# The feed-forward blocks of a group ahead of the output rows of the preceding group

## The reference

```
h = shift_token(x)
mu = h.mean(-1, keepdims=True)
var = h.var(-1, keepdims=True)
h = (h - mu) / jnp.sqrt(var + 1e-05) * lg + lb
h = h @ w1 + b1              # 256 -> 2 x 682
a, g = jnp.split(h, 2, axis=-1)
h = a * jax.nn.gelu(g, approximate=False)
x = x + h @ w2 + b2          # 682 -> 256
```

## Time and profile before

| | |
|---|---|
| median of 3 runs | 2665.61 us (2664.37 to 2666.09) |
| the profiled execution | 2666.19 us |
| its span, first to last instruction | 2664.4 us |
| mean granted TensorE clock, share of full speed | 0.992 |
| PE busy | 2590.7 us, 97% |
| DVE, ACT, POOL busy | 72%, 64%, 54% |
| feed-forward of layer 0 | about 1210 to 1608 us of the span |
| feed-forward of layer 1 | about 2264 us to the end |

### The profile page before, as it was taken

The page is one execution under the profiler, slowest core; times in us unless marked ns, Lnnn a source line. Parts: engine busy times, 40 slices in busy tenths (PEclk is TensorE's granted clock), DMA queues, the critical chain, the costliest instruction groups (busy, mean ns, idle before and its releaser), DMA issues.

```text
span 2664.4 us, 71388 instructions
## 1 busy us (share of the span) xinstructions
PE 2590.7 (97%) x25088; PEld 2225.2 (84%) x25088; DVE 1919.9 (72%) x3779; ACT 1703.1 (64%) x4184; POOL 1426.1 (54%) x1512
## 2 busy tenths in 40 slices
PE   7999999979999999999999998999999999999998
PEld 5888888768888888887888887888888888888887
DVE  7777777668888778786555556887788887666664
ACT  4666666658778777774444445877777877444442
POOL 7888888567777776662000006777777665000000
PEclk9999999989999999999999999999999999999999
DMA  2111111111111111112111111111111111222221
GB/s 48 37 48 38 43 38 35 42 45 39 50 41 47 41 39 38 57 50 70 56 49 59 53 36 43 40 49 41 49 39 39 40 59 36 79 76 74 78 77 40
DMA packets 167250, 130.39 MB, mean 49 GB/s; under 512 B 24870, under 2 KB 165320, under 8 KB 167093
## 3 DMA queue, kind: packets, MB, share of 16 engines
q1 hardware_dynamic: 164789, 119.81, 14.7%
q0 software_dynamic: 2304, 8.47, 1.1%
HBM read 77.47 MB, written 50.33 MB: 48 GB/s over the span
## 4 chain that ended last, share of the span: by engine, by line
PE 70%; DVE 12%; ACT 11%; issue 5%; POOL 1%; DMA 1%; DVEq 0%; ACTq 0%; SPq 0%; POOLq 0%
ACT attn_E L1103 8%; PE const_banks L1393 6%; PE const_banks L1394 6%; PE const_banks L1395 6%; PE const_banks L1401 3%; PE const_banks L1403 3%; PE const_banks L1402 3%; DVE attn_neg_top L1305 3%; DVE attn_ss L1295 3%; DVE attn_rot_b L1276 3%; PE const_banks L1416 3%; PE const_banks L1415 3%; PE const_banks L1414 3%; PE const_banks L510 3%; PE const_banks L525 3%
## 5 line engine op out<-in xcount | busy, mean ns | idle before, releaser
L1103 ACT ACTIVATE attn_E<-const_banks,attn_nbias,attn_rn 128x128 f32<-128x128 f32 x1024 | 453.5, 462 | 135.7 <-DVE attn_nbias L1310 135.7
L1014 POOL TENSOR_TENSOR attn_qk<-attn_rot_a,attn_rot_b 128x1024 f32<-128x1024 f32 x128 | 303.6, 2372 | 348.9 <-issue 296.7
L1001 POOL TENSOR_TENSOR ffn_rstd<-ffn_var,const_neg_half 128x4 f32<-128x4 f32 x32 | 32.3, 1010 | 669.5 <-DVE ffn_var L1200 669.5
L1401 PE MATMUL const_banks<-weights_w_hi,attn_xT_hi 128*128 128x512 f32 x768 | 316.2, 412 | 4.9 <-ACT attn_sq L1138 4.6
L1403 PE MATMUL const_banks<-weights_w_hi,attn_xT_lo 128*128 128x512 f32 x768 | 304.9, 397 | 0.0
L1402 PE MATMUL const_banks<-weights_w_lo,attn_xT_hi 128*128 128x512 f32 x768 | 304.6, 397 | 0.0
L1221 DVE SCALAR_TENSOR_TENSOR ffn_gated<-const_banks,weights_b_col,ffn_gate 128x512 f32<-128x512 f32 (+1 forms) x192 | 143.7, 748 | 213.7 <-ACT ffn_gate L1081 206.9
L1393 PE MATMUL const_banks<-ffn_xT_hi,ffn_w_hi 128*128 128x512 f32 x704 | 282.2, 401 | 3.4 <-DVE ffn_gated L1221 3.4
L1394 PE MATMUL const_banks<-ffn_xT_lo,ffn_w_hi 128*128 128x512 f32 x704 | 278.7, 396 | 0.0
L1395 PE MATMUL const_banks<-ffn_xT_hi,ffn_w_lo 128*128 128x512 f32 x704 | 278.3, 395 | 0.0
L1081 ACT ACTIVATE ffn_gate<-const_banks,weights_b_col 128x512 f32<-128x512 f32 x160 | 110.3, 689 | 217.4 <-PE const_banks L1395 217.1
(11 more groups left out here) (179 smaller groups left out, 8001.9 us busy)
## 6 DMA issues: line engine op xcount, KB each, us to landing
attn_x_res<-xa SPq DMA_DIRECT2D x128, 128.0 KB, 4.8
xb<-attn_x_new SPq DMA_DIRECT2D x128, 128.0 KB, 1.7
ffn_x_<-xb SPq DMA_DIRECT2D x128, 128.0 KB
h<-ident_h SPq DMA_DIRECT2D x64, 128.0 KB, 1.7
xa<-ident_n SPq DMA_DIRECT2D x64, 128.0 KB, 1.7
attn_x_<-xa SPq DMA_DIRECT2D x128, 64.0 KB
xa<-ffn_x_new SPq DMA_DIRECT2D x16, 512.0 KB, 3.3
ffn_add<-h SPq DMA_DIRECT2D x16, 512.0 KB, 5.0
```

Source lines behind the costliest of these rows:

```text
L1014: pool.tensor_tensor(qk[:, slot].rearrange("p a n -> p (a n)"), rot_a[:].rearrange("p a h d -> p (a h d)"), rot_b[:].rearrange("p a h d -> ...
L1103: last = act.activation(E[:, r, i], ps_s[:, r, i * P:(i + 1) * P], ACT.Exp, bias=nbias[:, r, i:i + 1], scale=rn[:, slot, h:h + 1], accum_o ...
L1401: pe.matmul(out_, xT_hi[:, slot, k], w.w_hi[:, k, cols], start=(k == 0), stop=False)
```

## The change

The output rows leave their places between the blocks, on PE and on DVE, and follow as a run of four behind the last block. Nothing else is moved: `group_turn` stays behind block 3, and ACT, POOL and SP keep their programs.

```
@@ forward_vector
             for p in range(KH):
-                if on(2) and 2 <= p < 2 + GROUP:
-                    row_done(dve, layer, t, i, u, p - 2)
                 if on(1):
                     if not (step == 1 and p == 0):
                         block_of(dve, layer, t, u, p)
...
             if on(1):
                 low_part(t, u, KH - 1)
+            for r in range(GROUP):
+                if on(2):
+                    row_done(dve, layer, t, i, u, r)
@@ forward_tensor
             for p in range(KH):
                 if on(1) and not (step == 1 and p < 2):
                     hidden(pe, layer, t, u, p)
-                if on(2) and 1 <= p <= GROUP:
-                    row_out(pe, t, u, p - 1)
...
                 if on(0) and step != 0 and p == XT_AT:
                     group_turn(pe, t)
+            for r in range(GROUP):
+                if on(2):
+                    row_out(pe, t, u, r)
             if layer < LAST and step == GROUPS:
```

## The result

Median 2688.34 us of four runs (2685.91 to 2690.75) against 2665.85 before; the ratio is 1.0086, 95% interval 1.0073 to 1.0099. The changed kernel is slower by 22.5 us, 0.84%. Its profiled execution took 2685.91 us, the lowest of the four, with a span of 2684.1 against 2664.4: +19.7. The trace is read against that. Ratios are of fast runs alone; one of the four runs of the kernel with the add ahead of low part 5 took 5527.75 us and is left out there.

What follows compares the result with a forecast made beforehand. PE, busy 97% of the span, was taken as the bound, so each new wait lengthens the kernel. 14.4 + 6.9 + 2.4 - 3.2 = +20.5 us gave a forecast of 2686 us (+0.77%), range 2675 to 2704.

Steps and rivals of the forecast that it cites:

- Behind the tail: Block 3, behind the tail block, waits for block 1's product: 0.48 us a step, 30 times, 14.4 us.
- The other blocks: Block 2, block 4 and the steady turn stay covered and cost nothing.
- The turn beside POOL: Steps 2 and 3 of layer 0: waits of 3.41 and 1.87 us, 1.66 of slow work after the first; 6.9 us.
- half microsecond less by the port rule: Turn, step 2 of layer 0: normalising would end no sooner than 1245.1, not 1245.55, making the sum half a microsecond less.
- Row 2 in layer 1: Row 2 waits for the two adds of row 0: 0.17 us in each of 14 steps, 2.4 us.
- a sign of being wrong: The prediction called itself wrong if block 3 waits for nothing, or if row 2 waits in layer 0 too.
- The end: Last group: 4.67 us of wait and slow row go, a 1.4 us wait for the store comes; net -3.2 us.
- hidden evictions: Block 3 and row 2 find their banks free; only +3.7 us remain, 2669.3 us; chance 0.08.
- a gain: Grouping saves switching between blocks and rows; only the end gains, at most 4.7 us; chance 0.04.
- the clock after short waits: Each half-microsecond wait brings a slow stretch like step 1's: 29 x 1.66 = 48 us, 2734; chance 0.03.
- The backlog: ACT and DVE fall behind blocks every 2.8 us, so row 2 waits in both layers: +22 us, 2708; chance 0.14.

Runs made afterwards that it cites:

- POOL's wait: The changed kernel, with POOL splitting weights only behind the four normalised rows in steps 1 to 3 of layer 0: 2677.25 us, ratio 1.0047.
- The single move: The kernel before, with output rows behind the blocks only in the last step of layer 1: 2661.82 us, ratio 0.9991.
- three cures: The kernel before, with rows behind the blocks in the last step only, tail as fourth block, POOL splitting weights behind the normalised rows: 2656.70 us, ratio 0.9970.

## Why the prediction was right

It said 2686 us; 2688.34 was measured, and on the profiled execution +20.5 against +19.7. By its terms:

- **Behind the tail, 0.48 us a step.** Measured 0.55 in layer 0 (24.82 against 24.27) and 24.78 against 24.27 in most single steps, 0.51. That this is the cover and nothing else, row 0 put back shows: 24.28. It fell in 29 steps and not in 30: step 16 of layer 0 has other work behind the tail.
- **The other blocks, nothing.** None waited in a steady step.
- **The turn beside POOL, 3.41 + 1.66 + 1.87.** Measured 3.34, 1.37 (1249.42 - 1244.38 = 5.04 against 3.67) and 1.84. The cause is shown by POOL's wait. That the stretch came to 7.8 us against 7.9 is in part luck: these three are 0.4 us less than forecast, and a wait of row 2 in step 3, 0.38 us as printed, was not in the sum. The four normalising instructions end 0.80 us behind POOL's subtraction, as they did before the change (1245.55 against 1244.76), and not 0.35, so the half microsecond less by the port rule did not come. The same rule (the Trainium skill, SBUF — State Buffer, Who interferes with whom) also says that an operation with two SBUF inputs contends with a GpSimd operation that reads SBUF; the trace agrees, since the low part of 3.86 us starts at 1237.92, inside POOL's subtraction, and ends at 1241.78, behind the subtraction's end at 1241.23.
- **Row 2 in layer 1, 0.17 us a step.** Measured 0.19 (24.97 against 24.78 with the add first). Its sum was off by 0.02: 3.13 + 0.45 + 0.42 is 4.00 and not 4.02. Row 2 also waited once in layer 0, in step 3. The prediction had named such a wait as a sign of being wrong, and on this point it was. There the slow normalisation put the tail's product, and with it the chain to the add, back: the adds start 10.6 us behind the turn (1282.94 - 1272.33) where a steady step has 9.65 and row 2 gives 10.5. It is one step of 14.
- **The end, -3.2.** The single move gives 3.2. The store landed in 3.0 us instead of 3.3, and the wait was 0.85 as printed, where 1 to 1.5 had been named; the two parts, 4.67 gained and 1.44 lost, were not measured apart.

The rivals: hidden evictions, a gain, and the clock after short waits fell with the first profile. The backlog did not occur in the steady steps of the change, but a wait of row 2 was nearer than its 0.14 suggests: with a short last block a step takes 1.3 us more than before in layer 0 (25.55) and 1.7 more in layer 1 (26.01). There it is not ACT and DVE that fall behind; the cover is shorter. The prediction took the distance from the last block to the adds from one row of step 1 and did not say what it hangs on; the run with the tail last showed that. Open is where the 1.2 us ahead of step 2 of layer 0 come from. Most of them lie in the attention work ahead of the feed-forward: PE waited there 3.2 us for `attn_qT` and 1.8 for `attn_tiny` before, 2.8 and 1.2 after, and no moved instruction stands ahead of either. The four runs of the changed kernel spread over 4.8 us and the four beside them over 2.5, but 18 other runs of the kernel before spread over 6.0, so this says nothing of the change.

## What to carry to other kernels

When PE is the bound and work is moved on it, ask of every piece what it covered: compare the chain that frees its banks (here 1.72 us of Gelu and product) with the shortest piece left in front of the waiting one (here 1.40 us), not with the average. A step of the same kernel that already runs without the moved work, such as the first of a pipeline, shows the new order before it is built; but name the start of each chain it shows, for its length holds only while the work between stays the same. And a piece of cover is worth its place more than its size: one row of four, put back between the tail and block 3, carried what the steady steps of layer 0 had lost.

## What the runs showed of the hardware that was not expected

POOL's subtraction of 3.50 us beside DVE stretched a low part, 42 partitions by 512 columns with both inputs in SBUF, from 0.69 to 3.86 us. A product of DVE of the same size, which reads PSUM, was not stretched: it took 0.74 us from 1221.02, inside POOL's subtraction from 1220.45 to 1224.29 (three cures on the kernel before). A wait of PE of 1.84 us left the granted clock at 1.00; one of 3.34 was followed by 7 us at 0.77, a part of them at 1.2 GHz, with the transposes of the turn at 1.97 us instead of 1.04.
